# First attention of a two-layer hybrid block: a new order on TensorE and VectorE, and 12 of 16 shared pieces ahead of the experts

## The reference

```python
x = x + attn_a(layernorm(x))     # one head of 128, softmax over the 256 tokens of a sequence
x = x + ffn(layernorm(x))        # layer 0: router, 8 experts, top 2, plus a shared expert
x = x + attn_b(layernorm(x))     # 16 heads of 8, masked
x = x + ffn(layernorm(x))        # layer 1, the same weights

def ffn(x):
    logits = x @ router_w                     # [4096, 8]
    combine, dispatch = top2_gating(logits, 1280)   # capacity 1280; positions by a running count
    expert_in = einsum('nec,nh->ech', dispatch, x)
    hmid = silu(expert_in @ w1 + b1)
    expert_out = hmid @ w2 + b2
    y = einsum('nec,ech->nh', combine, expert_out)
    shared = silu(x @ sw1 + sb1) @ sw2 + sb2
    return y + 0.1 * shared
```

## Time and profile before

| | |
|---|---|
| median of 3 runs | 835.18 us (833.74 to 836.4) |
| the profiled execution's own time | 834.34 us |
| its span, first to last instruction | 832.6 us |
| mean granted clock of PE | 0.969 of 2.4 GHz |

### The profile page before, as it was taken

One profiled execution on the slowest core, in us unless ns is written; L12 is line 12 of the kernel. 1 busy time (PEld: TensorE's weight loads), 2 busy tenths in 40 slices (PEclk: granted clock), 3 DMA queues, 4 the chain that ended last, 5 costly groups with the idle time before them and its releaser, 6 DMA issues. The chain is left out here.

```text
span 832.6 us, 18673 instructions
## 1 busy us (share of the span) xinstructions
PE 758.5 (91%) x6472; PEld 688.9 (83%) x6472; DVE 511.0 (61%) x1678; ACT 420.8 (51%) x1019; POOL 424.4 (51%) x519
## 2 busy tenths in 40 slices
PE   5787699799999997999999999999989599999994
PEld 4677689799999996777778787787779599999994
DVE  4687764254444466768787888867656344444437
ACT  2455445244444432755766666665655144444455
POOL 3247777155555550423444565665576255555530
PEclk9899979899999999999999999999999799999998
DMA  7981111233433134232223332233011233334138
GB/s 261 315 351 50 48 48 55 71 101 94 121 100 103 56 90 133 89 118 81 77 82 103 115 121 81 78 91 107 20 38 44 66 88 102 94 98 126 55 93 231
DMA packets 78164, 87.42 MB, mean 105 GB/s; under 512 B 12744, under 2 KB 66602, under 8 KB 77944
## 3 DMA queue, kind: packets, MB, share of 16 engines
q1 hardware_dynamic: 67872, 68.60, 26.9%
q0 software_dynamic: 9216, 17.34, 6.3%
q10 hardware_dynamic: 984, 0.29, 0.2%
HBM read 48.59 MB, written 39.65 MB: 106 GB/s over the span
## 5 line engine op out<-in xcount | busy, mean ns | idle before, releaser
L1145 ACT ACTIVATE hT<-bank,bias_T 128x256 f32<-128x256 f32 x448 | 175.4, 475 | 213.3 <-PE bank L788 213.2
L520 POOL DMA_INDIRECT y_rows<-yo,row_cur x160 | 157.6, 985 | 147.2 <-DVE yo L1608 120.4
L1698 DVE TENSOR_REDUCE negp<-bank 128x2 f32<-128x512 f32 (+1 forms) x192 | 128.1, 686 | 55.5 <-PE bank L852 52.9
L809 PE MATMUL bank<-w_s,hT 128*128 128x128 f32 x1280 | 155.9, 275 | 0.0
L809 PEld LDWEIGHTS bank<-w_s,hT 128*128 128x128 f32 x1280 | 150.0, 192 | 0.0
L558 POOL TENSOR_SCALAR_AFFINE_SELECT pt<-pt 128x512 f32<-128x512 f32 x128 | 79.5, 643 | 136.5 <-ACT pt L1205 136.4
L505 POOL DMA_INDIRECT x_slots<-xr,slot_u x128 | 128.8, 1006 | 39.5 <-issue 33.4
L1205 ACT ACTIVATE pt<-bank 128x512 f32<-128x512 f32 x192 | 107.7, 596 | 75.2 <-PE bank L880 62.8
L788 PE MATMUL bank<-xT_hl,w_hl 128*128 128x256 f32 x960 | 136.3, 292 | 3.3 <-DVE w_hl L1581 2.6
L788 PEld LDWEIGHTS bank<-xT_hl,w_hl 128*128 128x128 f32 x960 | 121.5, 193 | 4.0 <-DVE w_hl L1581 3.0
L1608 DVE TENSOR_TENSOR yo<-bank,b_b 128x256 f32<-128x256 f32 x80 | 34.0, 424 | 146.5 <-PE bank L809 146.5
(11 more groups left out here) (199 smaller groups left out, 1237.6 us busy)
## 6 DMA issues: line engine op xcount, KB each, us to landing
xg<-x_slots SPq DMA_DIRECT2D x80, 136.0 KB, 2.2
w_s<-in_L_ffn_w SPq DMA_DIRECT2D x32, 256.0 KB, 3.2
qk_rows<-qks SPq DMA_DIRECT2D x16, 512.0 KB, 4.3
bdk<-qk_rows SPq DMA_DIRECT2D x192, 32.0 KB
qc<-qk_rows SPq DMA_DIRECT2D x48, 128.0 KB, 2.8
x_slots<-xg SPq DMA_DIRECT2D x1, 5440.0 KB, 21.2
y_rows<-xg SPq DMA_DIRECT2D x1, 4096.0 KB, 15.0
bdk<-y_rows SPq DMA_DIRECT2D x1, 4096.0 KB
```

Of the source, the lines that this page charges most:

```text
L520: pool.indirect_dma_start(y_rows, bass.IndirectOffsetOnAxis(ap=row_cur[:, g % ROWS, j:j + 1], axis=0), yo[:, g % RING, j, :], None, bounds ...
L809: m = pe.matmul(yb(w, l)[:, j * P:(j + 1) * P], hT[:, w % 2, f, j * P:(j + 1) * P], wt[:, f, :], start=(f == 0), stop=(f == FT - 1))
L1145: a = act.activation(hT[:, w % 2, f, :], HB[2 * (w % 2) + f // 2][:, (f % 2) * 256:(f % 2) * 256 + 256], ACT.Silu, bias=bias_T[:, b0 + f:b ...
L1698: dve.tensor_reduce(dst, AB[(g + k) % 2][:, :].rearrange("p (j k) -> p j k", j=heads), AX.X, ALU.max, negate=True).then_inc(S.amax_done, 1)
```

## The change

- PE: `a_probs_transpose(n + 1)` now stands ahead of `r_transpose(i - 1)`, and `counts(i - 2)` behind `a_scores(n + 2)` and `a_project(n + 3)`.
- DVE: `second` and `norm_r` are interleaved from the start, so the four `norm_r` go in front of `add_attn(n)` and of the last four steps of `second`.
- DVE: `split_sw1` moves from the end of `i = 0` to the second half of `i = 6`, in front of `x_split`'s place and of `add_attn(n + 1)`.
- POOL: `DISPATCHED` goes from 7 to 11 and is halved where it is used: 2 + 11(i-2)//2 dispatches are issued ahead of iteration `i`'s `rstd2_of`, that is 29 ahead of the last one, not 37.
- `FRONT[0]` goes from 10 to 12: 12 pieces ahead of the chunks and 4 behind them. The `bias_add` of the tail follows it.

```diff
-FRONT = (10, 9)
+FRONT = (12, 9)
-DISPATCHED = 7
+DISPATCHED = 11
-                    upto = 2 + DISPATCHED * (i - 2)
+                    upto = 2 + DISPATCHED * (i - 2) // 2
# PE, attn_a_pair
-                if valid(i - 2):
-                    counts(i - 2, KK_)
+                if valid(i):
+                    a_probs_transpose(n + 1)
                 if valid(i - 1):
                     r_transpose(i - 1)
-                if valid(i):
-                    a_probs_transpose(n + 1)
                 if 0 <= n + 2 < SEQS:
                     a_scores(n + 2)
                 if 0 <= n + 3 < SEQS:
                     a_project(n + 3)
+                if valid(i - 2):
+                    counts(i - 2, KK_)
# DVE, attn_a_pair
+                for j in range(4):
+                    if valid(i - 2):
+                        second(i - 2, j)
+                    if valid(i - 1):
+                        norm_r(i - 1, j)
                 if valid(i - 2):
-                    for k in range(4):
-                        second(i - 2, k)
+                    second(i - 2, 4)
                 if valid(i):
                     add_attn(n)
-                for j in range(4):
-                    if valid(i - 2):
-                        second(i - 2, 4 + j)
-                    if valid(i - 1):
-                        norm_r(i - 1, j)
+                if valid(i - 2):
+                    for k in range(5, SECOND):
+                        second(i - 2, k)
+                if i == PAIRS - 2:
+                    split_sw1()
-                if i == 0:
-                    split_sw1()
# DVE, moe
-                    if c in (21, 26, 31):
-                        bias_add(l, 5 + (c - 21) // 5)
+                    if c in (21, 26, 31) and (FRONT[l] + 1) // 2 + (c - 21) // 5 < PAIRS:
+                        bias_add(l, (FRONT[l] + 1) // 2 + (c - 21) // 5)
```

## The result

The changed kernel takes 839.0 us (median of 8 runs, 837.32 to 846.67); the kernel before, beside it on the same chip, 835.42 (8 runs, 833.33 to 837.9). The ratio is 1.0065, 95% interval 1.0044 to 1.0086: slower by 0.65%, where I had put the likeliest case at 836.4 and within 0.3%. The medians alone give 1.0043: three of the eight runs are long, 841.51, 845.15 and 846.67. The profiled execution took 837.32, the shortest of the eight, with a span of 835.6; that is 3.0 above the 832.6 of the kernel before, and what follows explains these 3.0.

A forecast was written before the change was run, and what follows sets the result against it. Chunk 0 was taken to wait for POOL's last dispatch, not for PE. POOL +2.3, the two pieces -2.25 and the clock +1.2 sum to +1.25, giving 836.4 us against a median of 835.18; range 832.2 to 839.7.

The forecast's parts named there:

- the likeliest case: Whole kernel: 836.4 us, within 2.5 us of before; chance 0.56.
- The iteration: First attention: one iteration falls from 10.69 to 10.04 us, 0.65 less, with `norm_r` starting once `rstd2` ends.
- the attention: First attention, all iterations summed: it ends 7.9 us earlier, of which 5.3 from i=0 and i=1.
- Rival 1: First attention: `norm_r` need not wait for `rstd2`, so the sum is 2.8 less, 832.4; chance with rival 2 0.19.
- Rival 2: End of layer 0: rows return earlier, both pieces' 6.44 count, total -4.1, 831; chance with rival 1 0.19.
- Rival 4: First attention: PE waits for `norm_r` instead, iteration stays 10.69; +3.7, 838.9; chance with rival 3 0.25.
- Rival 3: End of layer 0: PE stays at 1.2 GHz from `b_transpose` to L851, +4.55, 839.7; chance with rival 4 0.25.
- the clock: Behind `keep_busy`, end of layer 0: PE idles 4.3 us, its clock falls, +1.2 (bounds 0 and +4.5).
- the two pieces: End of layer 0: two pieces fewer behind the chunks bring `combine` to `b_transpose` 2.25 us earlier, not 6.44.
- POOL: Ahead of chunk 0: 35 dispatches, not 27, behind the last scale; last one at 147.3, chunk 0 2.3 us later.
- the upper bound: POOL's dispatches behind the last scale: spacing of 1.32 us, the 35th at 147.7, +2.7.
- Chunk 0's stretch: PE from chunk 0 on: matmuls run at the low clock in both kernels, so nothing was added.

The follow-up runs named there:

- before_front12_b: The kernel before with 12 pieces ahead of the chunks and the change's `bias_add` lines, nothing else changed: 837.63 us, ratio 1.0036.
- front10_b: The changed kernel with 10 pieces ahead of the chunks instead of 12: 839.81 us, ratio 1.0049 to the kernel before.

## Why the prediction failed

**Right.** The iteration, 9.96 for 10.04, with `norm_r` bound by `rstd2`; no stall at `counts`; the attention 7.8 earlier in that execution, for 7.9; the gain given back by the dispatches behind the last scale; `combine` waiting for `yab`; a PE that idles in front of `b_transpose` (5.45, forecast 4) and works at the low level behind it. Rivals 1, 2 and 4 are refuted by those rows. Rival 3's total (839.7) is close to the median, and the range holds 839.0 only because of it; that is luck, for its mechanism is not what happened: the clock took 1.48 up to L851, not 4.5, and L788 is back at 1.70 at 317.63.

**The step that failed** is the sum: +2.3 - 2.25 + 1.2 = +1.25 for a measured 3.58 up to L851. The mechanisms stood and the terms were mis-sized, all in one direction, the two pieces most (half of the 2.25 was not there), then POOL.

- POOL, "I take 147.3, since the longer gaps are few": last dispatch 148.15, chunk 0 +2.97 for +2.3. The spacing is 1.333, above the upper bound that I had worked with. The 35 dispatches take 0.97 at the least, and the longest 1.37, 1.46 and 1.43 (at 104.19, 112.40 and 119.27). The Trainium skill (SBUF — State Buffer, section SBUF: two separate sides) says that the pair of ports that DVE and POOL share is locked by one instruction at a time; by that rule a dispatch beside a piece's cast could wait. The trace agrees in part: casts stand beside the first two of the three, none beside the one at 119.27, and the dispatches at 115.44 and 128.85 take 0.97 with a cast beside them. No run here takes the casts away, so the cause of the wider spacing stays open.
- The two pieces, -2.25: measured 2.10 - 3.22 = -1.12. The load starts 1.41 later behind the last scatter than I read from the earlier trace rows, held up by the instruction packet, and lands 0.23 faster.
- Chunk 0's stretch, "I add nothing": +0.25 (145.02 for 144.77).
- The clock, +1.2: measured +1.48.

2.97 + 0.25 - 1.12 + 1.48 = 3.58, the shift of L851; 0.6 came back behind it, within what the kernels differ there (505.7 to 508.1). One more reading was off and cost nothing: PE was to idle 7 to 8 in front of chunk 0 and idled 11.03, since the twelve pieces ended at 141.5, not near 144.

**And the start.** Forecast and comparison both rest on executions with an early start, which is worth 4.1 to the changed kernel up to i=2 and nothing to the kernel before. This fits its median lying 1.7 above its profiled 837.32, against 1.1 for the kernel before; the runs that make the median have no trace, so for them it is argued. The longest two, 845.15 and 846.67, lie 7.8 and 9.4 above the profiled one, more than the 4.1 of a late start; what they hold besides stays open. Nor is the old order free of such differences later on: its step from the scale of i=4 to that of i=5 was 10.69 in the kernel before and 11.6 in before_front12_b.

**What I should have compared.** The rows for it were there. Seven dispatches need 7 x 1.27 + 1.5 = 10.4 of POOL per iteration, so `DISPATCHED = 7` would have held the new iteration at 10.4 and not 10.0, five times 0.4 = 2 at the most (three times in the traces, 1.2); the change to 11/2 avoids these and pays eight dispatches at the end, 10. I priced the eight against the whole gain of the attention, and not against keeping them.

## What to carry to other kernels

When an engine's queue must be empty before the next stage can start, price a change by when its last instruction ends: letting it idle earlier, to spare another engine 0.4 us per turn, cost 10 us at the end here. Take the cheap half of a change alone: the new order with seven dispatches is what pays here, 828.68 us with ten pieces (0.9902 to 0.9955). Eleven pieces have the lowest ratio, 0.9876 (0.9839 to 0.9912), but their six runs spread from 820.03 to 832.86 and the intervals touch, so that they are better than ten is not shown. And before you book a gain at a stage's start, look at more than one execution: a wait can hide a start that varies, and the saving is then that of the lucky case.

## What the runs showed of the hardware

- Executions whose instructions are the same up to there differ in PE's clock in the first 26 us (the same two matmuls took 0.70 in the changed kernel and 1.22 us in front10_b), and so by 4.1 us in when the first statistics of i=0 start.
- 3.5 to 17.5 us without work on PE cost 2.5 to 3.2 us in the chunks behind (144.6 to 145.2 for 142.0 to 142.1), hardly more for 17.5 than for 3.5, and 5.45 us cost 1.5 to 1.8 in the second attention's start. The matmuls at the low level took 2.90 and 3.44 where they take 1.68 and 1.95 at the high one.
- A packet of instructions (16384 bytes, 0.93 to 1.53 us) beside the last scatter holds up the scatter's last data packet until it is over (0.01 to 0.02 us apart in five traces), and the load behind starts 1.1 to 2.0 us later (3.69 to 4.28 behind the scatter, for 2.32 to 2.55).
- Two chips took 884 to 885 us for a kernel that others run in 835 to 837, with gaps of up to 2.2 us in front of single matmuls that end in no semaphore.
